# Column-tiled filter products: four 32-column matmuls in place of one of 128, in steps of two filters

## The chip, the cores and the metric

The kernel runs on one core of a Trainium2 chip. The metric is the device time of one execution in microseconds (us). The kernel before was timed three times: 2059.23, 2060.93 and 2061.85 us, median 2060.93 us.

## What is computed

Two layers on an input of 4 x 56 x 56 x 128. Layer 0 is neighbourhood attention (7 x 7 windows, 4 heads) with an MLP. Layer 1 is a global attention of the form q * sum(k * v), then a spectral filter layer ("STU"): a causal FFT convolution of the tokens with 16 filters and a contraction with learned 128 x 128 matrices. The change is in this last part, whose core in the reference is

```
U_plus = jnp.fft.irfft(Vf[None, :, :, None] * Uf_p[:, :, None, :], n=n, axis=1)[:, :sl]
...
out = jnp.einsum('btkd,k,kde->bte', U_plus, s, Mpp)
out = out + jnp.einsum('btkd,k,kde->bte', U_minus, s, Mpm)
```

The kernel does it in the frequency domain. For each of 784 frequencies it forms a 128 x 128 filter matrix, a combination over the filter terms (118 rows: 16 filters times 7 Taylor terms, and 6 more) of spectra V and matrices M, and multiplies the token spectra U with it.

## The kernel before

The program has three parts in order of time: the front (layer 0, the global attention, forward DFT; lines up to 1160), the filter loop (class `Filters`, printed below) and the inverse DFT (class `Inverse`). Only the filter loop is touched.

The filter loop has 56 stages. Each stage has two kinds of work on TensorE (PE):

- **Filter products** (line 1262, `"filter"`): 64 products a stage. One takes a 118 x 128 bf16 slice of M as stationary operand (128 columns) and streams 224 columns of V. Four of them are one step; a step writes half of one of two (at the start four) double banks of PSUM, `pair(t)`. ScalarE (ACT, line 1298) empties the even steps and VectorE (DVE, line 1312) the odd ones, into the SBUF tensor `Gm`, 896 elements for each partition at a time. The next step on the same banks waits for that (`gm_act`, `gm_dve`).
- **Sums** (line 1279, `"sums"`): 28 items a stage, of four fp32 matmuls each, in column-tiled form: stationary operand of 32 columns, `tile_position=(0, 32 * x)`, output in 32 of the 128 PSUM partitions. The profile shows each of these fp32 matmuls as two LDWEIGHTS and two MATMUL instructions, each bf16 matmul as one and one.

The order on every engine is written out by `order()`: in eight blocks a stage, filter steps for stage s + 1 stand ahead of three or four sums of stage s. A block thus has 8 filter products (16 instructions) and on average 28 MATMUL instructions of the sums (56 instructions with their LDWEIGHTS). There are 448 blocks. The last stage has no filter steps beside its sums. PSUM banks 4 to 7 hold the sums; ACT copies them into `YS` (line 1304) after every second stage and SyncE stores them. GpSimd (POOL) prepares U (lines 1327 to 1339) two times in four stages.

[...]

Of the kernel before, what the change touches and what calls it, by code (L numbers as in the profile page):

```python
# [1068 lines left out]
class Spectrum:  # L1069
# [13 lines left out]
    def slot(self, i):  # L1083
        return self.psum[(2, 3, 4, 6)[i % 4]]
# [95 lines left out]
def load_spectra(e, D, S, c):  # L1180

    return e.dma_start(D["V"][c % 2].rearrange("k a (c x) -> k a c x", c=2),
                       D["VbD"][:, :, 2 * c:2 * c + 2, :].rearrange("a k c x -> k a c x")).then_inc(S[f"d_v{c % 2}"], 16)


def load_rows(e, D, S, c):

    if c in (0, 14):
        e.wait_ge(S["d_ud0" if c == 0 else "d_ud1"], 16 * NB)
    if c:  # L1190
        e.wait_ge(S["u7"], c)
    e.dma_start(D["UL"].rearrange("d b s x -> d b (s x)"), D["Ud"][:, :, FC * 8 * c:FC * 8 * c + FC * 8]).then_inc(S["d_ul"], 16)


def load_twiddles(e, D, S, c):
    return e.dma_start(D["TW"][c % 2][:, :, :], D["c_tw"][:, FC * c:FC * c + FC].rearrange("(o a) s -> o a s", o=1
                       ).broadcast_to([128, 3, FC])).then_inc(S[f"d_tw{c % 2}"], 16)


class Filters:  # L1200
# [15 lines left out]
    @staticmethod  # L1216
    def order():


        out = [("load", 0, 0), ("load", 1, 0), ("load", 2, 0)] + [("filter", 0, i) for i in range(16)]  # L1220
        last = Filters.STAGES - 1
        for s in range(last + 1):
            P = s // 4
            if s % 4 == 0 and P + 1 < NCH // 2:
                out += [("v_load", P + 1, 0), ("load", 2 * P + 3, 0)]
            if s % 4 == 3 and 2 * P + 4 < NCH:
                out.append(("load", 2 * P + 4, 0))
            if s > last - 4:
                out.append(("inverse", s - last + 3, 0))
            for j in range(8):  # L1230
                if s < last:
                    out += [("filter", s + 1, 2 * j), ("filter", s + 1, 2 * j + 1)]
                out += [("sums", s, i) for i in range(28 * j // 8, 28 * (j + 1) // 8)]
            if s % 2:
                out.append(("store", s // 2, 0))
        return out

    def pair(self, t):

        at = 1024 * (t % (4 if t < 16 else 2))  # L1240
        return self.banks[:, at:at + 1024].rearrange("p (e x) -> p e x", x=256)[:, :, 0:224]

    def tensor(self, e):
        S = self.S
        for k, s, i in self.order():
            P, half, par = s // 4, s // 2 % 2, s % 2
            if k == "filter":
                t = 16 * s + i
                if i == 0:
                    if s < 4:  # L1250
                        e.wait_ge(S[f"d_m{s}"], 16 * 9)
                    if s % 4 == 0:
                        e.wait_ge(S[f"d_v{P % 2}"], 16 * (P // 2 + 1))
                if t >= 16:
                    e.wait_ge(S["gm_dve" if t % 2 else "gm_act"], t // 2)
                elif t >= 4:
                    e.wait_ge(S["gm_dve" if t % 2 else "gm_act"], t // 2 - 1)
                pt = self.pair(t)
                if t == 1:
                    e.wait_ge(S["fu"], 8 * 2 * NB)  # L1260
                for q in range(4):
                    ins = e.matmul(pt[:, q, :], self.M[:, par, 64 * half + 4 * i + q, :], self.V[P % 2][:, par, :],  # L1262
                                   start=True, stop=True)
                ins.then_inc(S["gmm"], 1)
            elif k == "sums":
                gp, q = i // 2, (par, 2 + par)[i % 2]
                ch, bk = gp // 7, gp // 4
                p = self.banks[:, 2048 + 128 * gp:2176 + 128 * gp]
                if i == 0:
                    e.wait_ge(S["gm_act"], 8 * (s + 1))  # L1270
                    e.wait_ge(S["gm_dve"], 8 * (s + 1))
                if s % 4 == 0 and i in (0, 14):
                    e.wait_ge(S["u7"], 2 * P + ch + 1)
                if par == 0 and i % 8 == 0 and s >= 2:
                    e.wait_ge(S["ys"], 4 * (s // 2 - 1) + bk + 1)
                for x in range(4):
                    sl = 4 * (gp % 7) + x
                    r = 112 * ch + ((q // 2) * FC + sl) * 2
                    ins = e.matmul(p[32 * x:32 * x + 32, :], self.U7[(2 * P + ch) % 3][:, sl, 8 * (3 - q):8 * (3 - q) + 32],  # L1279
                                   self.Gm[:, par, r:r + 2, :], start=par == 0 and i % 8 == 0,  # L1280
                                   stop=par == 1 and i in (7, 15, 23, 27), tile_position=(0, 32 * x))
                ins.then_inc(S["sums"], 1)

    def evict_filter(self, e, s, i):
        t = 16 * s + i
        e.wait_ge(self.S["gmm"], t + 1)
        if s == 1 and i < 2:
            e.wait_ge(self.S["d_ud1"], 64)
        if s >= 2 and i < 2:
            e.wait_ge(self.S["sums"], 28 * (s - 1))  # L1290
        return self.Gm[:, s % 2, :, 4 * i:4 * i + 4], self.pair(t).rearrange("d e x -> d x e")

    def scalar(self, e):
        S = self.S
# [46 lines left out]
    def sync(self, e):  # L1341
        S, D = self.S, self.D
        for k, c, _ in self.order():
            if k == "v_load":
                if c >= 2:
                    e.wait_ge(S["gmm"], 64 * (c - 1))
                load_spectra(e, D, S, c)
            elif k == "load":
                if c >= 2:
                    e.wait_ge(S["u7"], c - 1)  # L1350
                    load_twiddles(e, D, S, c)
                if c:
                    load_rows(e, D, S, c)
            elif k == "store":
                e.wait_ge(S["ys"], 4 * c + 4)
                P, half = c // 2, c % 2
                for x in range(4):
                    e.dma_start(D["Yd"][56 * P:56 * P + 56].rearrange("(g s) r h x -> s r g h x", s=4)[x, :, :, half, :],
                                self.YS[32 * x:32 * x + 32, :, :]).then_inc(S["d_y"], 16)
            elif k == "inverse":  # L1360
                e.wait_ge(S["gmm"], 16 * (Filters.STAGES - 3 + c))
                if c < 2:
                    e.dma_start(D["IV"][c], D["c_inv"][:, c]).then_inc(S["d_iv"], 16)
                elif c == 2:
                    e.wait_ge(S["d_y"], 64 * (NCH // 2))
                    for a in range(4):
                        load_y(e, D, D["YL0"], a, 0, 0).then_inc(S["d_ylh"], 16)
                else:
                    e.wait_ge(S["d_y"], 64 * (NCH - 2))
                    for a in range(4, 7):  # L1370
                        load_y(e, D, D["YL0"], a, 0, 0).then_inc(S["d_yl0"], 16)
                    e.wait_ge(S["sums"], 28 * (Filters.STAGES - 1))
                    e.dma_start(D["rev"], D["c_rev"]).then_inc(S["d_rev"], 16)
        e.wait_ge(S["sums"], 28 * Filters.STAGES)
        load_out(e, D, S, 0)
        e.wait_ge(S["d_y"], 64 * NCH)
        load_y(e, D, D["YL0"], 7, 0, 0).then_inc(S["d_yl0"], 16)
        for a in range(8):
            load_y(e, D, D["YL1"], a, 0, 1).then_inc(S["d_yl1"], 16)
# [5 lines left out]
def load_y(e, D, yl, a, b, pp):  # L1385
    src = D["Yd"][G * a:G * a + G].rearrange("s (p r b) h x -> s b p r (h x)", r=2, b=4)[:, b, 2 * pp:2 * pp + 2]
    return e.dma_start(yl[a // 4][:, 1024 * (a % 4):1024 * (a % 4) + 1024].rearrange("s (p r x) -> s p r x", p=2, r=2), src)
# [8 lines left out]
def load_out(e, D, S, n):  # L1396

    for k in range(2):
        e.dma_start(D["RN"][n % 2][:, k], out_rows(D["T2"], n, k)).then_inc(S[f"d_rn{n % 2}"], 16)
# [290 lines left out]
```

## Time and profile before

| | |
|---|---|
| median of 3 runs | 2060.93 us |
| profiled execution | 2059.56 us, of which the span of the instructions is 2058.2 us |
| filter loop, first filter product to last sum | 990.6 to 1809.0 us of the span |
| PE busy | 1941.7 us (94%) |
| granted TensorE clock, mean | 0.976, in the filter loop 1.00 |

An engine's busy time counts what its instructions cover. MATMULs are pipelined, so a PE that is busy 100 of 100 us can still be passing through gaps; these show on PEld, the engine's record of the weight loads, as idle time with the reason in brackets. In the timeline rows, instructions of one line in a row are merged: start, duration to the end of the last one, count, and in brackets the idle time before them and what ended it. "issue" means that nothing the profile shows was waited for.

### The profile page before, as it was taken

Reading aid. Unit: us, or ns where it says so; the run is one execution under the profiler, and the core shown is the slowest. Engines: PE = TensorE matmul, PEld = TensorE weight load, DVE = VectorE, ACT = ScalarE, POOL = GpSimd, SP = SyncE. Lnnn points to the kernel's source line nnn. Section 1 sums busy time; section 2 is a strip of 40 time slices with the busy share of each in tenths; the row PEclk is TensorE's granted clock in tenths of the full one; section 3 lists DMA queues with packets and bytes.
Section 4 is the critical chain, followed back from the end, with each engine's and each line's share of the span. In section 5 each row is a group of like instructions: output and inputs, shape, how many; then the busy total and the mean of one; then the engine's idle time right before and its main releaser. Section 6 shows DMA issues by size and latency. Waiting matters only on the chain.

```text
span 2058.2 us, 64954 instructions
## 1 busy us (share of the span) xinstructions
PE 1941.7 (94%) x27483; PEld 1397.2 (68%) x27483; DVE 1163.5 (57%) x3209; ACT 1093.9 (53%) x2122; POOL 612.3 (30%) x780
## 2 busy tenths in 40 slices
PE   4899999989999888999999999999999999989998
PEld 2566666666666665665677777777777777767776
DVE  2567778878767653240465665665655656633332
ACT  4678887778766552222555555555555555500000
POOL 5344455555545430120422121222222121100000
PEclk8799999999999889999999999999999999999999
DMA  4332323323323223469322212221222112486651
GB/s 98 92 86 73 98 76 85 102 79 97 96 81 84 67 80 82 121 161 203 108 60 51 55 35 60 60 60 47 54 60 51 45 45 59 118 206 178 161 147 48
DMA packets 281600, 183.63 MB, mean 89 GB/s; under 512 B 55416, under 2 KB 279360, under 8 KB 279520
## 3 DMA queue, kind: packets, MB, share of 16 engines
q1 hardware_dynamic: 278942, 178.99, 33.5%
q8 instruction: 218, 3.57, 0.7%
q10 hardware_dynamic: 2304, 0.40, 0.2%
q14 instruction: 72, 0.59, 0.1%
q0 software_dynamic: 64, 0.08, 0.0%
HBM read 108.87 MB, written 70.63 MB: 87 GB/s over the span
## 4 chain that ended last, share of the span: by engine, by line
PE 75%; DVE 9%; issue 4%; POOL 4%; DMA 4%; ACT 3%; SPq 2%; DVEq 0%; POOLq 0%; ACTq 0%
PE banks L1279 19%; PE banks L1262 19%; PE banks L1444 10%; PE banks L1121 7%; PE banks L384 5%; PE banks L378 3%; DVE zone L583 2%; PE banks L343 2%; PE banks L333 2%; PE banks L357 2%; DVE st L570 1%; DMA W<-Un 1%; PE banks L391 1%; PE banks L431 1%; DVE W L623 1%
## 5 line engine op out<-in xcount | busy, mean ns | idle before, releaser
L1312 DVE COPY Gm<-banks 128x896 f32<-128x896 f32 x448 | 488.2, 1091 | 348.8 <-PE banks L1262 348.8
L1298 ACT ACTIVATE Gm<-banks 128x896 f32<-128x896 f32 x448 | 412.1, 920 | 318.7 <-PE banks L1262 314.1
L1262 PE MATMUL banks<-V,zone 118*128 118x224 bf16 x3584 | 438.1, 261 | 1.9 <-ACT qT L1133 0.6
L1279 PE MATMUL banks<-Gm,U 128*32 128x128 f32 x12544 | 434.9, 276 | 3.7 <-POOL U L1339 1.8
L1262 PEld LDWEIGHTS banks<-V,zone 118*128 118x128 bf16 x3584 | 291.9, 98 | 125.1 <-issue 44.8
L1279 PEld LDWEIGHTS banks<-Gm,U 128*32 128x32 f32 x12544 | 316.3, 110 | 85.2 <-issue 83.1
L1327 POOL COPY U<-UL 128x896 f32<-128x896 f32 x28 | 50.5, 1803 | 636.1 <-PE banks L1279 504.1
L1444 PE MATMUL banks<-YC,zone 98*98 98x256 f32 x1024 | 227.8, 381 | 1.3 <-DVE YC L1501 1.3
L1444 PEld LDWEIGHTS banks<-YC,zone 98*98 98x98 f32 x1024 | 169.8, 166 | 54.5 <-DVE YC L1501 1.8
L840 POOL TENSOR_TENSOR W<-W,mx 128x280 f32<-128x280 f32 x196 | 130.4, 666 | 229.6 <-DVE mx L630 229.5
L1121 PE MATMUL banks<-XR,W 98*128 98x392 f32 x512 | 175.5, 500 | 4.7 <-DVE W L1146 4.2
L343 PE MATMUL banks<-ident,W 128*98 128x128 f32 x784 | 125.2, 284 | 42.6 <-POOL W L840 25.4
L495 ACT ACTIVATE W<-W,mx 128x140 f32<-128x140 f32 x392 | 156.2, 402 | 0.3
L583 DVE TENSOR_SCALAR zone<-XR,zone 112x128 f32<-112x128 f32 x336 | 146.6, 481 | 16.6 <-DMA Un<-zone 9.4
L623 DVE CUSTOM_DVE_ANT_0 W<-banks,zone 128x140 f32<-128x140 f32 x392 | 102.8, 298 | 83.0 <-issue 40.9
L1121 PEld LDWEIGHTS banks<-XR,W 98*128 98x128 f32 x512 | 98.0, 193 | 74.6 <-DVE W L1146 4.5
L343 PEld LDWEIGHTS banks<-ident,W 128*98 128x98 f32 x784 | 87.7, 132 | 88.0 <-POOL W L840 51.6
L505 ACT ACTIVATE W<-banks 98x512 f32<-98x512 f32 x196 | 114.8, 586 | 46.1 <-PE banks L343 46.1
L1483 ACT ACTIVATE S<-banks 98x256 f32<-98x256 f32 x32 | 12.3, 384 | 229.5 <-PE banks L1444 229.5
L803 POOL TENSOR_TENSOR zone<-zone 112x4 f32<-112x4 f32 x112 | 119.7, 1069 | 9.3
L570 DVE BATCH_NORM_STATS2 st<-XR 112x6 f32<-112x128 f32 x448 | 107.4, 281 | 11.8 <-DMA XR<-in_x_dram 9.1
L384 PE MATMUL banks<-zone 128*112 128x128 f32 x896 | 106.1, 277 | 0.8 <-ACT zone L527 0.8
(142 smaller groups left out, 2275.7 us busy)
## 6 DMA issues: line engine op xcount, KB each, us to landing
Yd<-YS SPq DMA_DIRECT2D x112, 224.0 KB, 4.3
W<-Vd SPq DMA_DIRECT2D x392, 49.0 KB
UL<-Ud SPq DMA_DIRECT2D x28, 448.0 KB, 4.3
zone<-Yd SPq DMA_DIRECT2D x32, 392.0 KB
YL<-Yd SPq DMA_DIRECT2D x32, 392.0 KB
zone<-Mbf SPq DMA_DIRECT2D x28, 256.0 KB
Vd<-W SPq DMA_DIRECT2D x112, 56.0 KB
T<-XR SPq DMA_DIRECT2D x28, 224.0 KB, 3.2
```

Source lines behind the costliest of these rows:

```text
L343: ins = e.transpose(self.psum[4][0:G, 256 * c + 128 * j:256 * c + 128 * j + 128], self.PN[n % 3][:, j, G * c:G * c + G], self.ident[:, :])
L384: ins = e.matmul(p[0:TB, 128 * m:128 * m + 128], self.HT[:, f, TB * m:TB * m + TB], self.wf2[:, f, :], start=f == 0, stop=f == 3)
L495: ins = e.activation(self.PB[n % 3][:, j, :], self.SB[n % 3][:, j, :], ACT.Exp, bias=self.mx[n % 4][:, j:j + 1], scale=-1.0, accum_out=sel ...
L570: ins = v.bn_stats(self.st[:, m, :], self.row(g)[:, 128 * m:128 * m + 128])
L583: ins = v.tensor_scalar(x[:, m, 0:128], self.row(g)[:, 128 * m:128 * m + 128], self.mv[k][g % 2][:, m, 0:1], self.rs[k][g % 2][:, m:m + 1] ...
L840: q.tensor_tensor(self.inner(self.PN[n % 3]), self.PB[n % 3], r, ALU.mult).then_inc(S["pn"], 1)
L1121: ins = e.matmul(p[:, 0:392], src[:, a, 128 * m:128 * m + 128], self.F[:, c, a, 392 * half:392 * half + 392], start=a == 0, stop=a == 3)
L1262: ins = e.matmul(pt[:, q, :], self.M[:, par, 64 * half + 4 * i + q, :], self.V[P % 2][:, par, :], start=True, stop=True)
L1279: ins = e.matmul(p[32 * x:32 * x + 32, :], self.U7[(2 * P + ch) % 3][:, sl, 8 * (3 - q):8 * (3 - q) + 32], self.Gm[:, par, r:r + 2, :], st ...
L1298: e.activation(dst, src, ACT.Copy).then_inc(S["gm_act"], 1)
L1312: v.tensor_copy(dst, src).then_inc(S["gm_dve"], 1)
L1444: ins = e.matmul(p[0:G, 256 * c:256 * c + 256], self.D["IV"][c][:, a, G * jt:G * jt + G], self.YC[n % 2][:, int(k), a], start=a == 0 and ( ...
```

## The change

Each filter product of 118 x 128 is made of four matmuls with a stationary operand of 32 columns, each at its own column tile, as the sums have it. A step is now two filters (8 matmuls) instead of four (4 matmuls), writes one PSUM bank of four by turns (eight at the start), and each emptying copies 448 elements for each partition instead of 896. There are twice as many steps, waits and emptying instructions.

```
-                out += [("filter", s + 1, 2 * j), ("filter", s + 1, 2 * j + 1)]
+                out += [("filter", s + 1, 4 * j + i) for i in range(4)]
...
-    def pair(self, t):
+    def slot(self, t):
-        at = 1024 * (t % (4 if t < 16 else 2))
-        return self.banks[:, at:at + 1024].rearrange("p (e x) -> p e x", x=256)[:, :, 0:224]
+        at = 512 * (t % (8 if t < 32 else 4))
+        return self.banks[:, at:at + 512].rearrange("p (e x) -> p e x", x=256)[:, :, 0:224]
...
-                if t >= 16:
-                    e.wait_ge(S["gm_dve" if t % 2 else "gm_act"], t // 2)
-                elif t >= 4:
-                    e.wait_ge(S["gm_dve" if t % 2 else "gm_act"], t // 2 - 1)
+                if t >= 8:
+                    e.wait_ge(S["gm_dve" if t % 2 else "gm_act"], (t - (4 if t >= 36 else 8)) // 2 + 1)
...
-                for q in range(4):
-                    ins = e.matmul(pt[:, q, :], self.M[:, par, 64 * half + 4 * i + q, :], self.V[P % 2][:, par, :],
-                                   start=True, stop=True)
+                for q in range(2):
+                    for x in range(4):
+                        ins = e.matmul(pt[32 * x:32 * x + 32, q, :], self.M[:, par, 64 * half + 2 * i + q, 32 * x:32 * x + 32],
+                                       self.V[P % 2][:, par, :], start=True, stop=True, tile_position=(0, 32 * x))
...
-        return self.Gm[:, s % 2, :, 4 * i:4 * i + 4], self.pair(t).rearrange("d e x -> d x e")
+        return self.Gm[:, s % 2, :, 2 * i:2 * i + 2], self.slot(t).rearrange("d e x -> d x e")
```

The other edits only rescale counts (16 steps a stage become 32).

How PE's program reads in the middle of a stage, before. Each row is a matmul as the program has it, so the sums stand with half of the profile's count; two steps of four products, then sums:

```order
L1262 MATMUL banks<-V,zone 128x224 [waits gm_act]
L1262 MATMUL banks<-V,zone 128x224 x3
L1262 MATMUL banks<-V,zone 128x224 [waits gm_dve]
L1262 MATMUL banks<-V,zone 128x224 x3
L1279 MATMUL banks<-Gm,U 32x128 x16
```

And the same place after the change (the lines have moved up by one):

```order
L1261 MATMUL banks<-V,zone 32x224 [waits gm_act]
L1261 MATMUL banks<-V,zone 32x224 x7
L1261 MATMUL banks<-V,zone 32x224 [waits gm_dve]
L1261 MATMUL banks<-V,zone 32x224 x7
L1261 MATMUL banks<-V,zone 32x224 [waits gm_act]
L1261 MATMUL banks<-V,zone 32x224 x7
L1261 MATMUL banks<-V,zone 32x224 [waits gm_dve]
L1261 MATMUL banks<-V,zone 32x224 x7
L1278 MATMUL banks<-Gm,U 32x128 x16
```

Eight matmuls with two waits have become 32 with four; the sums behind them are the same.

On ACT, around the copies into `YS` at the end of an odd stage and in the next, before:

```order
L1304 ACTIVATE YS<-banks 128x256 [waits d_y,sums]
L1298 ACTIVATE Gm<-banks 128x224x4 [waits sums,gmm]
L1298 ACTIVATE Gm<-banks 128x224x4 [waits gmm] x7
L1298 ACTIVATE Gm<-banks 128x224x4 [waits sums,gmm]
L1298 ACTIVATE Gm<-banks 128x224x4 [waits gmm] x2
L1304 ACTIVATE YS<-banks 128x512 [waits d_y,sums]
```

And after:

```order
L1297 ACTIVATE Gm<-banks 128x224x2 [waits sums,gmm]
L1297 ACTIVATE Gm<-banks 128x224x2 [waits gmm] x15
L1297 ACTIVATE Gm<-banks 128x224x2 [waits sums,gmm]
L1297 ACTIVATE Gm<-banks 128x224x2 [waits gmm] x5
L1303 ACTIVATE YS<-banks 128x512 [waits d_y,sums]
L1297 ACTIVATE Gm<-banks 128x224x2 [waits gmm] x4
```

Each copy into `Gm` is half as large and there are two for one; the copy into `YS` stands at the same place between blocks. DVE changes in the same way, without `YS`.

## Rows read from the trace of the kernel before

**Rows 1.** The page: engines' busy time, share of the span and instructions

```profile
PE 1941.7 (94%) x27483; PEld 1397.2 (68%) x27483; DVE 1163.5 (57%) x3209; ACT 1093.9 (53%) x2122; POOL 612.3 (30%) x780
```

**Rows 2.** The page, costliest groups: busy, mean ns of one, idle before

```profile
L1312 DVE COPY Gm<-banks 128x896 f32<-128x896 f32 x448 | 488.2, 1091 | 348.8 <-PE banks L1262 348.8
L1298 ACT ACTIVATE Gm<-banks 128x896 f32<-128x896 f32 x448 | 412.1, 920 | 318.7 <-PE banks L1262 314.1
L1262 PE MATMUL banks<-V,zone 118*128 118x224 bf16 x3584 | 438.1, 261 | 1.9 <-ACT qT L1133 0.6
L1279 PE MATMUL banks<-Gm,U 128*32 128x128 f32 x12544 | 434.9, 276 | 3.7 <-POOL U L1339 1.8
```

**Rows 3.** The filter products' line: duration min/median/max, first and last start

```profile
L1262 PE MATMUL banks<-V,zone x3584: 257/259/271, 991.0 to 1799.4; 118*128 118x224 bf16 x200
```

**Rows 4.** The sums' line, the same columns

```profile
L1279 PE MATMUL banks<-Gm,U x12544: 269/273/299, 1001.4 to 1809.0; 128*32 128x128 f32 x200
```

**Rows 5.** Timeline of PE in the middle of the filter loop

```profile
1401.46 0.94 PE L1262 MATMUL banks<-V,zone 118*128 118x224 bf16 x8
...
1404.08 1.08 PE L1279 MATMUL banks<-Gm,U 128*32 128x128 f32 x32
1405.09 0.94 PE L1262 MATMUL banks<-V,zone 118*128 118x224 bf16 x8
```

**Rows 6.** Timeline of PEld, the weight loads, in the same stretch

```profile
1402.33 0.59 PEld L1279 LDWEIGHTS banks<-Gm,U 128*32 128x32 f32 x24 [0.18 <-issue]
1403.12 0.31 PEld L1262 LDWEIGHTS banks<-V,zone 118*128 118x128 bf16 x4 [0.20 <-ACT Gm L1298]
1403.59 0.31 PEld L1262 LDWEIGHTS banks<-V,zone 118*128 118x128 bf16 x4 [0.15 <-DVE Gm L1312]
```

**Rows 7.** Timeline of PEld in the front: fp32 alone, full and tiled forms

```profile
224.60 0.27 PEld L357 LDWEIGHTS banks<-W 98*32 98x32 f32 x16 [0.18 <-issue]
224.96 0.18 PEld L333 LDWEIGHTS banks<-kP,qT 32*32 32x32 f32 x16
225.36 0.39 PEld L297 LDWEIGHTS banks<-ident,W 112*128 112x128 f32 x4 [0.22 <-issue]
...
226.76 0.13 PEld L343 LDWEIGHTS banks<-ident,W 128*98 128x98 f32 x1 [0.71 <-issue]
```

**Rows 8.** Timeline of PEld, last stage of the loop: sums alone

```profile
1800.89 4.54 PEld L1279 LDWEIGHTS banks<-Gm,U 128*32 128x32 f32 x165 [0.50 <-issue]
1807.34 1.67 PEld L1279 LDWEIGHTS banks<-Gm,U 128*32 128x32 f32 x59 [1.91 <-issue]
```

**Rows 9.** DMA queues, whole span: packets, MB, share of 16 engines

```profile
q8 instruction: 218, 3.57, 0.7%
```

**Rows 10.** DMA queues in the filter loop, 1030 to 1790 us

```profile
q1 hardware_dynamic: 74470, 40.07, 21.2%
q8 instruction: 118, 1.93, 1.1%
```

**Rows 11.** DMA queues that start in 1804.5 to 1804.6 us

```profile
q1 hardware_dynamic: 19, 0.02, 97.0%
q8 instruction: 1, 0.02, 80.1%
```

**Rows 12.** DMA queues that start in 1808.9 to 1808.95 us

```profile
q8 instruction: 1, 0.02, 109.5%
```

**Rows 13.** DMA queues that start in 1767.2 to 1767.3 us

```profile
q8 instruction: 1, 0.02, 70.1%
```

**Rows 14.** DMA queues that start in 1771.1 to 1771.2 us

```profile
q8 instruction: 1, 0.02, 64.4%
```

**Rows 15.** Groups by shape, ACT, 1020 to 1790 us

```profile
L1304 ACT ACTIVATE YS<-banks 128x512 f32<-128x512 f32 x81 | 48.2, 595 | 9.6 <-PE banks L1279 7.8
L1304 ACT ACTIVATE YS<-banks 128x256 f32<-128x256 f32 x27 | 10.4, 384 | 15.0 <-PE banks L1279 15.0
```

**Rows 16.** Groups by shape, DVE, a smaller copy out of PSUM

```profile
L655 DVE COPY zone<-banks 128x129 f32<-128x129 f32 x4 | 1.1, 279 | 1.2 <-PE banks L391 1.2
```

More of the change, by code:

```diff
@@ L1217, in order @@
     def order():
-        out = [("load", 0, 0), ("load", 1, 0), ("load", 2, 0)] + [("filter", 0, i) for i in range(16)]
+        out = [("load", 0, 0), ("load", 1, 0), ("load", 2, 0)] + [("filter", 0, i) for i in range(32)]
         last = Filters.STAGES - 1
@@ L1247, in tensor @@
             if k == "filter":
-                t = 16 * s + i
+                t = 32 * s + i
                 if i == 0:
@@ L1253, in tensor @@
                         e.wait_ge(S[f"d_v{P % 2}"], 16 * (P // 2 + 1))
-                if t >= 16:
-                    e.wait_ge(S["gm_dve" if t % 2 else "gm_act"], t // 2)
-                elif t >= 4:
-                    e.wait_ge(S["gm_dve" if t % 2 else "gm_act"], t // 2 - 1)
-                pt = self.pair(t)
-                if t == 1:
+                if t >= 8:
+                    e.wait_ge(S["gm_dve" if t % 2 else "gm_act"], (t - (4 if t >= 36 else 8)) // 2 + 1)
+                pt = self.slot(t)
+                if t == 2:
                     e.wait_ge(S["fu"], 8 * 2 * NB)
-                for q in range(4):
-                    ins = e.matmul(pt[:, q, :], self.M[:, par, 64 * half + 4 * i + q, :], self.V[P % 2][:, par, :],
-                                   start=True, stop=True)
+                for q in range(2):
+                    for x in range(4):
+                        ins = e.matmul(pt[32 * x:32 * x + 32, q, :], self.M[:, par, 64 * half + 2 * i + q, 32 * x:32 * x + 32],
+                                       self.V[P % 2][:, par, :], start=True, stop=True, tile_position=(0, 32 * x))
                 ins.then_inc(S["gmm"], 1)
@@ L1269, in tensor @@
                 if i == 0:
-                    e.wait_ge(S["gm_act"], 8 * (s + 1))
-                    e.wait_ge(S["gm_dve"], 8 * (s + 1))
+                    e.wait_ge(S["gm_act"], 16 * (s + 1))
+                    e.wait_ge(S["gm_dve"], 16 * (s + 1))
                 if s % 4 == 0 and i in (0, 14):
@@ L1284, in evict_filter @@
     def evict_filter(self, e, s, i):
-        t = 16 * s + i
+        t = 32 * s + i
         e.wait_ge(self.S["gmm"], t + 1)
@@ L1345, in sync @@
                 if c >= 2:
-                    e.wait_ge(S["gmm"], 64 * (c - 1))
+                    e.wait_ge(S["gmm"], 128 * (c - 1))
                 load_spectra(e, D, S, c)
@@ L1360, in sync @@
             elif k == "inverse":
-                e.wait_ge(S["gmm"], 16 * (Filters.STAGES - 3 + c))
+                e.wait_ge(S["gmm"], 32 * (Filters.STAGES - 3 + c))
                 if c < 2:
```

## The prediction

> **What bounds the kernel now.** I began with the busy times. PE is busy 94% of the span, DVE 57% and ACT 53% [rows 1]. The costliest groups come next: the filter products and the sums each cover some 435 us of PE, and the two engines that empty PSUM wait for the filter products 349 and 319 us [rows 2]. The first product starts at 991.0 and the last sum at 1809.0 and lasts 0.27 us, so the filter loop takes 818.3 us [rows 3, 4], and PE sets its pace.
>
> PE is not at its best there. The timeline shows two blocks, from 1401.46 to 1405.09, so 1.815 us a block [rows 5]; 448 blocks make 813 us, the rest is the start and the end. What should a block take? Eight products cover 0.94 us, of which the last is 0.26 us, so they follow each other every (0.94 - 0.26) / 7 = 0.097 us [rows 2, 5], eight in 0.78 us. The sums at full flow are in the last stage: 165 weight loads take 4.54 us and 59 take 1.67 us; the difference, in which the length of the last one drops out, gives (4.54 - 1.67) / 106 = 27 ns each [rows 8]; 28 take 0.756 us. Together 1.533 us. The missing 0.28 us stands beside the weight loads: 0.18 us idle before the sums, 0.20 us before the products, 0.15 us between the two product steps [rows 6].
>
> **What the change removes.** Are the first two idles a matter of the form of the matmuls or of bf16 against fp32? The front answers: with fp32 alone, the weight loads idle 0.18 us from the full form to the tiled one and 0.22 us back, and not at all from one tiled line to the next (L357 to L333) [rows 7]. So it is the form, and the change, which gives both kinds the tiled form, removes both. The third idle is a wait for DVE to empty the banks. With four banks by turns a step waits for the copy of four steps before, which is a whole block old, so that should go too. Streaming costs the same: four tiled fp32 matmuls of 128 columns start within 4 x 27 = 108 ns, which shows that four tiles run side by side, and a tiled product still streams 224 columns once. I take 0.097 us for it, the row of the same 224 columns; the other bound is the 108 ns of a tiled group, 0.09 us a block or 40 us in all. [...] By this part alone the loop would lose 448 x 0.282 = 126 us.
>
> **What it adds: instructions.** A bf16 matmul is one weight load and one MATMUL. The products go from 2 x 3584 = 7168 to 28,672 instructions; the sums keep 25,088 [rows 2]. The loop grows from 32,256 to 53,760. A block of 64 + 56 = 120 instructions in 1.533 us needs one every 12.8 ns, for 818 us on end; before it was one every 25 ns.
>
> Can PE be fed at this rate? The instruction queue brought 218 packets of 3.57 MB in all, 16.4 KB each [rows 9]; PE's 54,966 matmul instructions [rows 1] divided by 218 are 252, and with the waits, which the page does not count, some 256: one packet is one page of 256 PE instructions. In the loop 118 came in 760 us, one in 6.4 us [rows 10], 256 x 25 ns. After the change a page lasts 256 x 12.8 = 3.27 us.
>
> The last stage already runs at this density, since nothing but sums is left: 330 instructions at 13.5 ns. And there PE stops: after 165 loads it is idle for 1.91 us, put down to "issue", no semaphore [rows 8]. A page fetch starts in 1804.5 to 1804.6 and takes 80.1% of 16 engines for 0.1 us, which is 1.28 us [rows 11]. It ends at about 1805.85, after PE's last load (1805.43), and PE goes on at 1807.34, 1.5 us later. The next fetch starts at 1808.9 to 1808.95 [rows 12]. I read this as two pages of room: the next page is asked for when the sequencer enters the one before. The front has a smaller stop of the same look, 0.71 us of "issue" in the middle of four like transposes [rows 7].
>
> A starved PE thus gets one page for each round of asking, fetching and starting. That round was 4.3 to 4.45 us here, under DMA engines 97% taken [rows 11]. In the loop the data queues take 21% [rows 10], and the closest two fetches that I found start in 1767.2 to 1767.3 and 1771.1 to 1771.2 [rows 13, 14]: 3.8 to 4.0 us; a round can't be longer than that there. Both ends lie above the 3.27 us that PE needs, so the loop will go at the pace of the fetches. Between them I take 4.1 us, nearer to the lighter traffic but above it, since that pair is the closest of many. 53,760 / 256 = 210 pages x 4.1 = 861 us, which is 43 us more than 818.3. At 3.8 us it is 798 (20 less), at 4.45 us 935 (116 more). The gain of 126 us is inside this: it only lets PE reach the starvation sooner.
>
> **The copies.** Copies of 896 elements become twice as many of 448. ACT: 595 ns for 512 elements and 384 for 256 give 0.82 ns an element and 0.17 fixed, so 0.54 us each, 1.08 us a block, and with `YS` ((48.2 + 10.4) us over 425 blocks = 0.14) 1.22 us [rows 15]. DVE: 1091 ns for 896 and 279 for 129 elements [rows 2, 16] give 1.06 ns an element and 0.14 us fixed, 0.62 us each, 1.23 us a block. (With no fixed part 1.09, the lower bound.) Both fit beside 1.53 us of PE and more so beside 120 / 256 x 4.1 = 1.92 us. They cost nothing as long as PE or its feeding is the bound; without that cover the loop would be at 1.23 us a block. The doubled waits sit on weight loads and on copies; SyncE and POOL have their old order with rescaled counts.
>
> **Sum.** 2059.56 + 43 = 2103 us in the profiled execution. The median of the runs is 1.4 us above that execution, which is less than the 0.2% (4 us) that I count as no change; I say 2103.
>
> **Rivals.**
> (1) Feeding does not limit: the stop in the last stage came only from the crowded DMA engines, and a quiet round is under 3.3 us. Then 2059.6 - 126 = 1934 us, or 1974 with 108 ns a product. For it: 97% against 21% of DMA share. Against it: fetches are no closer than 3.8 us, though nothing in the loop asked for them faster, so this is weak evidence. The packet itself takes only 1.03 to 1.13 us there [rows 10, 14]; the rest is asking and starting, which I saw only in the crowd. [...] Chance 0.17.
> (2) Feeding limits, but with rounds of 3.5 to 3.85 us: 735 to 809 us for the loop, 1976 to 2050 us. This is the case if a part of the 1.5 us between a fetch's end and PE's restart was the crowd's doing. It decides at 818.3 / 210 = 3.90 us: below that the change gains. Chance 0.17.
> (3) Rounds near 3.9 us: within 0.2%. Chance 0.05.
> (4) The forecast, rounds of 3.95 to 4.45 us: 2071 to 2176 us. Chance 0.52.
> (5) Rounds beyond 4.45 us, since the transfers of `Yd` and `UL` crowd the engines in bursts: over 2176 us. Chance 0.09.
>
> Faster 0.34, same 0.05, slower 0.61. The range: leaving out (1) at the low end and part of (5) at the top gives 1975 to 2185; the forecast's own is 2071 to 2176.
>
> **What the changed profile would show.** PEld idle of 0.18 to 0.22 us between products and sums gone, products and sums flowing at 24 to 27 ns an instruction pair. Stops of PE of 0.5 to 1.3 us with "issue" every 256 instructions, at places that drift through the program, with no semaphore. The instruction queue with 84 packets more, about 302, and in the loop one each 3.9 to 4.4 us. A block of 1.9 us on average. DVE copies of 0.62 us, ACT of 0.54 us. The prediction is wrong if the stops are absent (1), if PE waits for DVE or ACT at the products, or if tiled bf16 products take clearly over 108 ns.

## The result and the profile after

The changed kernel takes 2089.98 us (median of 4 runs, 2085.39 to 2092.91), the kernel before 2061.39 us in the same series: ratio 1.0136, 95% interval 1.0113 to 1.0159. It is slower by 28.6 us.

The page of the changed kernel, with the rows that answer to [rows 1, 2, 9] and the chain of work that ended last:

```profile
PE 1873.7 (90%) x38235; PEld 1481.3 (71%) x38235; DVE 1213.7 (58%) x3657; ACT 1177.7 (56%) x2570; POOL 613.8 (29%) x780
...
q8 instruction: 302, 4.95, 1.0%
...
PE 71%; issue 9%; DVE 8%; DMA 4%; POOL 3%; SPq 3%; ACT 2%; DVEq 0%; POOLq 0%; ACTq 0%
...
L1311 DVE COPY Gm<-banks 128x448 f32<-128x448 f32 x896 | 538.8, 639 | 325.5 <-PE banks L1261 324.6
L1297 ACT ACTIVATE Gm<-banks 128x448 f32<-128x448 f32 x896 | 508.0, 636 | 275.7 <-PE banks L1261 273.5
L1278 PE MATMUL banks<-Gm,U 128*32 128x128 f32 x12544 | 488.6, 275 | 54.4 <-issue 48.6
L1261 PE MATMUL banks<-V,zone 118*32 118x224 bf16 x14336 | 492.7, 261 | 49.3 <-issue 46.1
```

PE is busy less (90% instead of 94%), though it has 10,752 matmuls more; "issue" has become 9% of the chain (4% on the page before); and PE's idle time beside the two lines of the loop, next to nothing before, is 104 us, nearly all of it "issue". The instruction queue, q8, has 84 packets more, 302, of 16.4 KB each (4.95 MB / 302). PE has 2 x 10,752 = 21,504 instructions more, matmuls and weight loads, and 21,504 / 84 = 256 for each packet more.

The loop goes from the first product at 996.9 us to the end of the last sum at 1842.8 us, 845.9 us against 818.3. The other 5.9 us of the difference between the two profiles lie ahead of the loop, where the two programs are the same: in the twelve profiled kernels of this study the first product starts anywhere from 991.0 to 999.2 us.

PE's timeline in the middle of the loop, the rows at two stops:

```profile
1401.72 0.75 PE L1278 MATMUL banks<-Gm,U 128*32 128x128 f32 x19 [0.83 <-issue]
...
1402.39 0.76 PE L1261 MATMUL banks<-V,zone 118*32 118x224 bf16 x24
...
1403.17 0.94 PE L1278 MATMUL banks<-Gm,U 128*32 128x128 f32 x27
...
1406.03 0.32 PE L1278 MATMUL banks<-Gm,U 128*32 128x128 f32 x4 [0.81 <-issue]
```

The stops are in the midst of the sums, where nothing is waited for. How many instructions lie between two of them? Busy time of PE, PEld, DVE, ACT and POOL in the stretches between three stops, with the counts in brackets, and behind them the granted clock, the DMA share and GB/s:

```profile
1401.70:1406.01 4.31, 3.49 (x128) 3.23 (x128) 2.38 (x4) 2.22 (x4) 0.00 (x0) 1.00 0.19 41
1406.01:1409.76 3.75, 3.49 (x128) 3.23 (x128) 2.22 (x4) 2.21 (x4) 0.00 (x0) 1.00 0.02 4
```

Both times 128 weight loads and 128 MATMULs, 256 instructions, in 4.31 and 3.75 us, in each of which PE is busy 3.49 us. That is one packet of the instruction queue, the page of the prediction. The DMA queues of packets that start in 1403.5 to 1403.6 us:

```profile
q8 instruction: 1, 0.02, 54.9%
```

and in 1407.1 to 1407.2 us:

```profile
q8 instruction: 1, 0.02, 72.2%
```

The first takes 54.9% of 16 engines for 0.1 us, 0.88 us, so it ends at about 1404.45, and PE goes on at 1406.03, 1.6 us later. Then 1.1 us pass to the start of the next fetch. So each stretch reads: PE restarts, the next page is fetched, and some 1.4 us after its end PE restarts again. The records of the whole stretch from 1030 to 1790 us say the same: there are 160 gaps of more than 0.25 us between the starts of PE's instructions, 126 us in all, and each lies 128 matmuls behind the one before, sometimes 127, or a small multiple of that (a matmul is two instructions; a few waits among them are not counted). For these 160 the time from a fetch's end to the restart behind it is 1.19 to 1.60 us, median 1.39; from the restart to the start of the next fetch 1.06 to 4.2 us, median 1.17, mean 1.51. The queues of this stretch:

```profile
q1 hardware_dynamic: 73955, 38.17, 20.3%
q8 instruction: 192, 3.15, 1.7%
```

192 fetches in 760 us are one in 3.96 us, and 1.7% of 16 engines are 1.08 us for each. 1.51 + 1.08 + 1.39 = 3.98 us: the three parts, two of them taken over the 160 pages with a stop, make up the whole round.

### The profile page after: what moved, and what is told of

The parts are those of the page before. It is cut to its first block, busy times and chain, and to the rows that moved or that the text cites. A ratio compares the mean times of both kernels' runs of the same rounds, so it can differ in the third digit from the quotient of the medians.

```text
span 2091.6 us, 87354 instructions
## 1 busy us (share of the span) xinstructions
PE 1873.7 (90%) x38235; PEld 1481.3 (71%) x38235; DVE 1213.7 (58%) x3657; ACT 1177.7 (56%) x2570; POOL 613.8 (29%) x780
## 3 DMA queue, kind: packets, MB, share of 16 engines
q8 instruction: 302, 4.95, 1.0%
## 4 chain that ended last, share of the span: by engine, by line
PE 71%; issue 9%; DVE 8%; DMA 4%; POOL 3%; SPq 3%; ACT 2%; DVEq 0%; POOLq 0%; ACTq 0%
PE banks L1278 18%; PE banks L1261 17%; PE banks L1443 10%; PE banks L1121 7%; PE banks L384 5%; PE banks L378 3%; PE banks L343 2%; DVE zone L583 2%; PE banks L333 2%; DMA Ud<-kP 2%; PE banks L357 2%; DVE st L570 1%; PE banks L391 1%; PE banks L431 1%; DVE W L623 1%
## 5 line engine op out<-in xcount | busy, mean ns | idle before, releaser
L1311 DVE COPY Gm<-banks 128x448 f32<-128x448 f32 x896 | 538.8, 639 | 325.5 <-PE banks L1261 324.6
L1297 ACT ACTIVATE Gm<-banks 128x448 f32<-128x448 f32 x896 | 508.0, 636 | 275.7 <-PE banks L1261 273.5
L1278 PE MATMUL banks<-Gm,U 128*32 128x128 f32 x12544 | 488.6, 275 | 54.4 <-issue 48.6
L1261 PE MATMUL banks<-V,zone 118*32 118x224 bf16 x14336 | 492.7, 261 | 49.3 <-issue 46.1
L1261 PEld LDWEIGHTS banks<-V,zone 118*32 118x32 bf16 x14336 | 396.8, 97 | 78.6 <-issue 71.8
L1278 PEld LDWEIGHTS banks<-Gm,U 128*32 128x32 f32 x12544 | 387.5, 111 | 76.2 <-issue 71.8
L1443 PEld LDWEIGHTS banks<-YC,zone 98*98 98x98 f32 x1024 | 170.5, 167 | 54.9 <-DVE YC L1500 1.6
```

What stands on the lines that cost most here:

```text
L1261: ins = e.matmul(pt[32 * x:32 * x + 32, q, :], self.M[:, par, 64 * half + 2 * i + q, 32 * x:32 * x + 32], self.V[P % 2][:, par, :], start= ...
L1297: e.activation(dst, src, ACT.Copy).then_inc(S["gm_act"], 1)
L1311: v.tensor_copy(dst, src).then_inc(S["gm_dve"], 1)
L1443: ins = e.matmul(p[0:G, 256 * c:256 * c + 256], self.D["IV"][c][:, a, G * jt:G * jt + G], self.YC[n % 2][:, int(k), a], start=a == 0 and ( ...
```

## The experiments

All ratios are to the kernel before, run on the same chip. "Loop" is from the first product to the end of the last sum in the profiled execution, "round" the loop divided by its page fetches. The expectations name three theories. A: PE is starved by the page fetches. B: the smaller steps, with more waits and smaller copies, cost the time. C: a tiled bf16 product is slow in itself, whatever the fetches do.

| kernel | us | ratio, 95% interval | loop | fetches in it | round |
|---|---|---|---|---|---|
| before | 2061.39 | | 818.3 | 126 | 6.49 |
| changed | 2089.98 | 1.0136, 1.0113 to 1.0159 | 845.9 | 210 | 4.03 |
| bank part alone | 2050.67 | 0.9935, 0.9909 to 0.9961 | 803.9 | 126 | 6.38 |
| form alone | 2084.27 | 1.0092, 1.0061 to 1.0122 | 841.3 | 210 | 4.01 |
| 64-column tiles | 2055.52 | 0.9964, 0.9944 to 0.9984 | 813.1 | 154 | 5.28 |
| three tiles of four | 1985.85 (one run) | | 741.6 | 182 | 4.07 |
| two tiles of four | 1939.86 (one run) | | 702.2 | 154 | 4.56 |
| matmuls cut in halves | 2483.02 (one run) | | 1238.1 | 322 | 3.85 |
| changed, more DMA traffic | 2131.98 (one run) | | 885.7 | 210 | 4.22 |
| before, more DMA traffic | 2069.25 | 1.0016, 0.9997 to 1.0036 | 824.1 | 126 | 6.54 |
| mixed 1:1 | 1998.93 | 0.9697, 0.9671 to 0.9723 | 755.6 | 168 | 4.50 |
| mixed 2:1 | 1999.73 | 0.9691, 0.9663 to 0.9719 | 758.6 | 182 | 4.17 |

The fetches are those that the traces show from the loop's start to its end. They are to the unit the loop's matmuls and weight loads divided by 256 (53,760 / 256 = 210).

**The two halves of the change.** First the bank part alone, the changed kernel with

```
-                    for x in range(4):
-                        ins = e.matmul(pt[32 * x:32 * x + 32, q, :], self.M[..., 32 * x:32 * x + 32], ..., tile_position=(0, 32 * x))
+                    ins = e.matmul(pt[:, q, :], self.M[:, par, 64 * half + 2 * i + q, :], self.V[P % 2][:, par, :],
+                                   start=True, stop=True)
```

> The bank part of the change alone: products in the full 128-column form again, but in steps of two filters in one of four banks, with copies of 448 elements. Theory A (PE is starved by the page fetches): 32,256 loop instructions as before, so no starvation; the form switches stay; only the wait for DVE between the product steps goes, 0.08 us in every second block of the trace before, some 18 us: about 2043 us. Theory B (smaller steps, more waits and smaller copies cost the time): slower than before, up to the 2090 us of the changed kernel.

It gained: ratio 0.9935, some 13 us, where some 18 were expected. Its weight loads:

```profile
1399.99 0.69 PEld L1260 LDWEIGHTS banks<-V,zone 118*128 118x128 bf16 x8 [0.20 <-ACT Gm L1296]
1400.87 0.81 PEld L1277 LDWEIGHTS banks<-Gm,U 128*32 128x32 f32 x32 [0.18 <-issue]
1401.88 0.69 PEld L1260 LDWEIGHTS banks<-V,zone 118*128 118x128 bf16 x8 [0.20 <-issue]
```

The idle between the product steps [rows 6] is gone: eight loads are now always in one row. The idles at the changes of form are as before. Theory B, that the small steps cost the time, falls.

Then the form alone, the kernel before with

```
                 for q in range(4):
-                    ins = e.matmul(pt[:, q, :], self.M[:, par, 64 * half + 4 * i + q, :], ...)
+                    for x in range(4):
+                        ins = e.matmul(pt[32 * x:32 * x + 32, q, :], self.M[..., 32 * x:32 * x + 32], ..., tile_position=(0, 32 * x))
```

> The form alone: tiled products, 53,760 loop instructions, but steps of four filters, two double banks and copies of 896 elements as before. Theory A: the loop goes at the pace of the fetches whatever the banks do, as the changed kernel within 10 us, 2080 to 2100 us. Theory B: the loss came with the small steps, so this one is well under 2061 us, about 1950.

2084.27 us: nearly the whole loss is there without the small steps. Its weight loads and waits:

```profile
1401.38 0.87 PEld L1280 LDWEIGHTS banks<-Gm,U 128*32 128x32 f32 x32
1402.24 0.41 PEld L1263 LDWEIGHTS banks<-V,zone 118*32 118x32 bf16 x16
1402.84 0.31 PEld L1263 LDWEIGHTS banks<-V,zone 118*32 118x32 bf16 x16 [0.20 <-DVE Gm L1313]
1403.14 0.66 PEld L1280 LDWEIGHTS banks<-Gm,U 128*32 128x32 f32 x24
```

```profile
PEld banks L1263 <- DVE Gm L1313: 91.3, 346, 0.4
PEld banks L1280 <- issue: 31.6, 43, 1.8
...
PEld banks L1263 <- issue: 17.7, 29, 3.0
```

From sums to products and back nothing idles any more. But PE now waits 91 us for DVE from 1000 to 1800 us, and "issue" is 49 us there, instead of 132 in the same stretch of the changed kernel. The waits cost nothing in the sum, which I read so: while PE waits for DVE, the next page arrives, and a loop that is paced by the fetches takes the same time whichever wait fills the round. Why this kernel is a shade better than the changed one (a loop of 841.3 us against 845.9) is not shown; its granted clock was 0.50 for 10 us of the loop, the changed kernel's for 24 (last section).

**Fewer instructions at the same streaming.** In the changed kernel the fourth tile (`x` in `range(3)`), then the third and fourth (`range(2)`) are left out after the first eight steps, so a quarter or half of each product is missing. The tiles run side by side, and PE needs as long for two as for four: the weight loads of eight products and of 32 matmuls of the sums take 1.66 us with two tiles (from 1400.10 us in that trace), and 1.65 with four (from 1026.52 us in the changed kernel, where no stop falls in).

> The changed kernel without the fourth of the four column tiles of each product (it is left out after the first eight steps, so a quarter of the products is missing). The remaining three still stream 224 columns side by side, so PE's array needs as long; there are 104 instructions a block, 46,600 in the loop, 182 pages. Theory A: 182 pages at some 4.15 us (PE itself needs 3.77 us a page), 755 us for the loop, about 2000 us in all. Theory C with a cost that is the array's or the copies' and not the instruction's: unchanged, 2090 us.

> The changed kernel with only two of the four column tiles of each product (after the first eight steps; half of the products is missing). 88 instructions a block, 154 pages, no change of form. Theory A: PE needs 4.46 us a page, few rounds are longer, 4.6 us on average: a loop of 709 us, about 1950 us in all, and hardly any stop. It is the time that tiling would give if PE were fed. Theory C: above 2000 us.

1986 and 1940 us, with 7136 and 14,272 instructions less. The expectations were about 2000 and 1950. With two tiles "issue" is all but gone; the waits for the sums' line, and none of this kind for the products', from 1000 to 1690 us:

```profile
PEld banks L1278 <- issue: 3.5, 2, 3.1
```

against these two rows of the changed kernel, from 990 to 1840 us:

```profile
PEld banks L1261 <- issue: 71.8, 102, 3.6
PEld banks L1278 <- issue: 69.6, 84, 2.4
```

The loop with two tiles, 702.2 us, is 1.567 us a block: the 1.533 us that the prediction worked out for a fed PE, and 2%.

**More instructions at the same streaming.** Each tiled matmul of 224 columns becomes two of 112:

```
                 for q in range(2):
-                    for x in range(4):
-                        ins = e.matmul(pt[32 * x:32 * x + 32, q, :], ...
+                    for y in range(2):
+                        for x in range(4):
+                            ins = e.matmul(pt[32 * x:32 * x + 32, q, 112 * y:112 * y + 112], ...
```

> The changed kernel with each tiled matmul's 224 columns cut into two of 112: the same columns streamed and the same results, but 28,672 instructions more, 82,432 in the loop, 322 pages. Theory A: 322 rounds of 3.96 us, a loop of 1275 us, 2520 us in all, with a stop at each page as before. Theory C (a cost of each product or copy): hardly more than 2090 us; a cost of some 11 ns for each matmul on PE itself: 2250 us.

2483 us, 393 more than the changed kernel and 37 less than expected. PE's timeline, the rows with a stop in 10 us:

```profile
1400.31 0.28 PE L1262 MATMUL banks<-V,zone 118*32 118x112 bf16 x8 [1.63 <-issue]
...
1404.33 0.97 PE L1262 MATMUL banks<-V,zone 118*32 118x112 bf16 x64 [1.42 <-issue]
...
1408.08 0.58 PE L1262 MATMUL banks<-V,zone 118*32 118x112 bf16 x32 [1.51 <-issue]
```

The stops are as far apart as before, 3.8 to 4.0 us, only longer (in the mean 1.61 us from 1030 to 2200 us, 0.79 in the changed kernel), since PE gets through a page sooner. With halves, with all four tiles and with three, the loop is the number of pages times a round of 3.85 to 4.07 us; with two tiles the round is shorter than what PE needs for a page (4.46 us, of 4.56 measured). The line is not exact. With three tiles PE needs 3.77 us a page and stops for more than 0.25 us only 52 times in the 741.6 us of the loop; it is starved in bursts. And the halves have a shorter round than the changed kernel: their data queues take 14.1% of the DMA engines (from 1030 to 2200 us), the changed kernel's 20.3%.

**Traffic on the data queues.** After each store a copy of 0.8 MB from memory to memory:

```
+                if c:
+                    e.wait_ge(S["d_junk"], 16 * c)
+                e.dma_start(D["junk"]..., D["x"]...[0:28]).then_inc(S["d_junk"], 16)
```

> The changed kernel with one more DMA for each store, 28 in the loop, that copies 0.8 MB from one place in memory to another and that nothing waits for until the next store: 22.5 MB on top of 40. Theory A: a page fetch that falls into it is late, and PE with it: 20 to 60 us more than the changed kernel, 2110 to 2150 us. If the round's length doesn't hang on the data queues: unchanged, 2090 us.

> The control to the traffic run: the same 28 additional copies of 0.8 MB, put into the kernel before, where a page lasts 6.4 us. Theory A: a fetch that is late by one or two us is still in time, so the kernel before stays at 2061 us within 5 us. If the copies cost in another way (SyncE's queue, the stores or loads of the loop), it is slower by about the same 40 us as the changed kernel was.

The changed kernel rose to 2132 us in its one run, by 42; the kernel before to a ratio of 1.0016, which the measurement does not tell from none. So the round depends on the data traffic (4.22 us with the copies, 4.03 without), and here that counted only where the pages are short: in the kernel before a page has 6.54 us with the copies and 6.49 without. The waits of the changed kernel with the traffic:

```profile
PEld banks L1278 <- issue: 99.0, 84, 3.8
...
PEld banks L1261 <- issue: 73.9, 91, 3.8
```

84 and 91 times where it was 84 and 102, and each longer in the mean. Read as in the section on the result, the part of the round that grew is the one from PE's restart to the start of the next fetch: in the mean 1.84 us (1.51 without the traffic), against 1.05 for the fetch (1.08) and 1.39 from its end to the restart (1.39).

**Which change of form costs?** The products in two tiles of 64 columns, `pt[64 * x:64 * x + 64, q, :]`, `tile_position=(0, 64 * x)`:

> Each product as two matmuls of 64 columns instead of four of 32; all else as in the changed kernel. 88 instructions a block, 39,424 in the loop, 154 pages; at 1.53 us a block a page lasts 4.46 us, longer than most rounds. Theory A, if changing between 64- and 32-column tiles costs nothing: 154 pages at about 4.6 us, a loop of 709 us, 1953 us in all. Theory A, if it costs what full against tiled costs (0.25 us a block): 1.78 us a block, about 2040 us. Theory C (a tiled bf16 product is slow in itself, whatever the fetches): at or above the changed kernel's 2090 us.

2055.52 us, 15 above what was expected if this change of width costs what the other does. Its weight loads:

```profile
1400.75 0.72 PEld L1261 LDWEIGHTS banks<-V,zone 118*64 118x64 bf16 x16 [0.20 <-issue]
1401.64 0.59 PEld L1278 LDWEIGHTS banks<-Gm,U 128*32 128x32 f32 x24 [0.17 <-issue]
1402.43 0.72 PEld L1261 LDWEIGHTS banks<-V,zone 118*64 118x64 bf16 x16 [0.20 <-ACT Gm L1297]
```

From 64 to 32 columns the loads idle 0.17 us and back 0.20 us, as dear as full and tiled (0.18 and 0.20): with equal widths side by side, as in the rows of the form alone, none of these idles is there. With 5.28 us a page the fetches are out of it, and the loop is 9 us longer than with the bank part alone, which has the same idles. Most of this is in the products: from the first product's weight load to the first sum's it takes 0.888 us here and 0.873 there, in the mean of some 400 blocks from 1020 to 1740 us, and 448 x 0.015 = 6.7 us. The stretch of the sums is the same in both, 0.903 us. Theory C falls here too, since the tiled bf16 products cost no more than that.

**A version between.** If the form of a block decides both its instructions and its changes of form, half of each may be better than all of one:

```
                 for q in range(2):
+                    if i // 4 % 2:
+                        ins = e.matmul(pt[:, q, :], self.M[:, par, 64 * half + 2 * i + q, :], self.V[P % 2][:, par, :],
+                                       start=True, stop=True)
+                    else:
...
```

> The changed kernel with every second block's products in the full form again (steps 4 to 7 of each 8), the others tiled. A pair of blocks has 120 + 72 = 192 instructions and one change of form there and one back: PE alone needs 2 x 1.533 + 0.25 = 3.31 us for it, 4.4 us a page, longer than the mean round of 3.96 us of the changed kernel's trace, though not than all. Theory A (page fetches): about 4.6 us a page, 3.43 us a pair, a loop of 770 us against some 800 for the kernel with the bank part alone (2051 us): about 2020 us, faster than both. Theory C (tiled bf16 products cost by themselves): between 2051 and 2090 us.

1998.93 us, ratio 0.9697 (0.9671 to 0.9723), 3.0% faster than the kernel before. The expectation was 2020, 21 us more. The loop has the 168 pages it should and takes 755.6 us instead of 770, 4.50 us a page instead of 4.6, which is 14 us of it; the other 7 were not looked for (the spread of the front is up to 8). Weight loads over two blocks:

```profile
1400.17 0.69 PEld L1261 LDWEIGHTS banks<-V,zone 118*128 118x128 bf16 x8 [0.20 <-ACT Gm L1302]
1401.04 0.81 PEld L1283 LDWEIGHTS banks<-Gm,U 128*32 128x32 f32 x32 [0.18 <-issue]
1401.84 0.80 PEld L1265 LDWEIGHTS banks<-V,zone 118*32 118x32 bf16 x32
1402.62 0.67 PEld L1283 LDWEIGHTS banks<-Gm,U 128*32 128x32 f32 x24
1403.48 0.59 PEld L1261 LDWEIGHTS banks<-V,zone 118*128 118x128 bf16 x7 [0.20 <-ACT Gm L1302]
```

One change of form there and one back for two blocks, and the 32 tiled loads begin as soon as the sums' end. They take from 1401.84 to 1402.62, eight products in 0.78 us or 0.097 each, as in the full form.

With two blocks tiled for one full (`if t // 4 % 3 == 2:`):

> As the mixed kernel, but two blocks tiled for one in full form instead of one for one. 312 instructions in three blocks with one change of form there and back; PE alone needs 4.84 us for them, 3.97 us a page, as long as the mean round. Theory A: more pages wait than in the mixed kernel, and it gains less from the changes of form: 1999 us within 10 us.

1999.73 us. More pages (182), fewer changes of form, the same time: the optimum is flat there.

## Why the prediction was right

- **What bounds the kernel, and the gain of 126 us for a fed PE.** Right. The idles at the changes of form are gone in every kernel that has 32-column tiles throughout, and the kernel with two tiles shows the loop at 1.567 us a block. That kernel's copies are as many as the changed one's, so they fit beside PE. A tiled bf16 product costs 0.097 us, the bound I chose (the mixed kernel's rows). The other bound, the 108 ns of a tiled fp32 group, is not what the trace shows: the four loads of a product take 97 ns.
- **The instructions.** Right: 84 packets more, 210 pages in the loop, 256 PE instructions each. The 252 and "some 256" of the kernel before hold: its trace has 808 instructions of PE's sequencer, 807 of them waits, and (54,966 + 808) / 218 = 255.8. The growth between the two kernels (21,504 / 84) and the stretches between two stops give 256. One phrase was wrong and had no consequence: at 12.8 ns each the loop's instructions last 53,760 x 12.8 ns = 688 us, not "818 us on end".
- **Two pages of room, one page for each round.** The stops every 256 instructions, the constant time from a fetch's end to the restart, and the line of times against pages show that a starved PE gets one page a round. More room than two pages does not fit [rows 8, 10]: the kernel before left most of its 6.4 us a page without a fetch (one takes 1.1 us), and still PE ran dry after 330 instructions in the last stage. That the request is made on entering a page is still my reading of the order of events; no run separates it from other schemes that keep one fetch under way.
- **The round.** I took 4.1 us; the loop divided by its pages is 4.03. On 210 pages this is 15 us, the whole of what the loop's growth was forecast too large (43 us, measured 27.6), and about what the median of 2090 us lies under the forecast of 2103 us. That it came so close is in part luck: 4.1 was a choice between 3.8 and 4.45, and the direction hung on it, since the change gains below 3.90. The halves, starved at nearly every page, even went at 3.85. The crowd in the last stage had not made the restart slow, as rival (2) needed: the 1.5 us from [rows 8, 11] is within the 1.19 to 1.60 us in the middle of the loop. What more traffic does lengthen is the time until a fetch starts, 1.84 us in the traffic run against 1.51.
- **The copies.** That they fit beside PE was right, the size was off: ACT takes 636 ns where I had 540, DVE 639 where I had 620. PE's weight loads for the products waited for them 4.8 us in all in the loop, against 71.8 us of "issue".
- **Rivals.** (1) is refuted: the mean round is 4.03 us. Single ones are shorter than the 3.88 us of the closest pair before; the closest two fetches in this loop start 3.28 us apart, so that pair was no lower limit. And with the data queues at 20.3%, not 97%, PE still has 160 stops of more than 0.25 us from 1030 to 1790 us. (5) did not come about with this traffic, but the traffic run goes its way, with a mean round of 4.22 us.

## What to carry to other kernels

Count PE's instructions for each microsecond before splitting matmuls: here a stream denser than 256 instructions in some 4 us (16 ns each) starves, and splitting paid only down to that density (two blocks of three tiled 1999.73 us, one of two 1998.93). A change of tile width idled the weight loads for 0.17 to 0.22 us each way, so order the work to have few of them; where instructions and changes of width pull against each other, mix the forms. A stop of "issue" in the middle of like instructions, 256 instructions or a multiple of it behind the one before, was a page fetch in these traces; the instruction queue's packets tell.

## What was not expected of the hardware

The granted clock dropped in the changed kernel's loop, where it had been 1.00 throughout. The busy time of PE, PEld, DVE, ACT and POOL in the first 100 us and, behind it, the granted clock (0.95), the DMA share and GB/s:

```profile
1000.00:1100.00 100.00, 86.66 (x3030) 80.30 (x3025) 64.02 (x109) 63.56 (x119) 37.66 (x35) 0.95 0.25 69
```

In the loop's 846 us the granted clock was 0.50 for 24 us in all and 1.00 otherwise; with the halved matmuls, whose stops are twice as long, it was 0.50 for 72 us. In the changed kernel each of the six pieces begins 0.2 to 1.4 us after one of the longest stops: PE's last start before it and the next are 2.2 to 3.6 us apart, where the mean stop has 0.8. Seven stops of 2.1 to 3.0 us have no piece beginning behind them. Two stretches of 32 weight loads of the products, the first at a granted clock of 0.50, the second at 1.00:

```profile
1010.76 1.53 PEld L1261 LDWEIGHTS banks<-V,zone 118*32 118x32 bf16 x32
1026.52 0.80 PEld L1261 LDWEIGHTS banks<-V,zone 118*32 118x32 bf16 x32
```

From these two rows, 1.53 us against 0.80, 24 us at 0.50 did the work of some 12, and by this estimate the low clock cost at most 12 us of the loop. It does not explain the loss by itself: without it the loop would still be 16 us longer than before. How much of the 12 is hidden in the rounds was not measured.

ACT's copies into `Gm` write runs of two elements where they wrote runs of four. With a fixed 0.17 us [rows 15], an element took 0.83 ns in runs of four (920 ns for 896) and 1.03 ns in runs of two (636 for 448). Whether the run's length is the cause was not tried.
